# A GRU with a ternary feed-forward network: half group sums ahead of the transposes, a bias seed from ScalarE, and another division of the last tile but one

## The reference, cut to what matters

```python
gi = x @ W_ih + b_ih;  gh = h @ W_hh + b_hh
r = sigmoid(i_r + h_r);  z = sigmoid(i_z + h_z)
n = tanh(i_n + r * h_n)
h_new = (1.0 - z) * n + z * h
...
scale = clip(mean(abs(w_g)), 1e-08)          # groups of 64
w_hat = clip(round(w_g / scale), -1, 1) * scale
gate, up = split(states @ w_gate_up_hat)     # hidden size 1024
h = silu(gate) * up
hn = h * rsqrt(mean(h * h) + eps)            # over the 1024 hidden features
out = x + hn @ w_proj_hat
```

## Time and profile before

| what | us |
|---|---|
| median of 3 runs (354.89 to 356.31) | 355.58 |
| the profiled execution | 355.06 |
| its span, first to last instruction | 353.2 |
| PE busy in the span | 343.9 (97%) |
| DVE busy | 230.1 (65%) |
| ACT busy | 212.8 (60%) |
| POOL busy | 172.5 (49%) |
| the lone steps, transposes of step 0 to those of step 7 | 38.0 |

### The profile page before, as it was taken

How to read it: one execution, slowest core, us unless ns; L and a number is a source line. 1 busy time by engine, 2 the same in 40 slices (tenths; PEclk the granted TensorE clock), 3 DMA queues, 4 the chain that set the end, 5 groups by cost and what they waited for, 6 DMA issues and landing times.

```text
span 353.2 us, 5445 instructions
## 1 busy us (share of the span) xinstructions
PE 343.9 (97%) x2026; PEld 298.5 (84%) x2031; DVE 230.1 (65%) x438; ACT 212.8 (60%) x408; POOL 172.5 (49%) x144
## 2 busy tenths in 40 slices
PE   7999999999999999999999999999999999999994
PEld 3788887888888888888888889888898888898894
DVE  6788887899666655656648554675656545744655
ACT  4776767876747566456646656366565556645651
POOL 1022121176735447255363447445462556889882
PEclk9999999999999999999999999999999999999999
DMA  6990000017001000220001000010001000010101
GB/s 226 385 416 16 2 1 2 0 45 314 1 2 59 0 3 1 75 105 1 2 0 61 0 2 0 0 62 1 2 0 59 2 0 2 1 59 2 59 2 60
DMA packets 5570, 17.92 MB, mean 51 GB/s; under 512 B 420, under 2 KB 2084, under 8 KB 5032
## 3 DMA queue, kind: packets, MB, share of 16 engines
q1 hardware_dynamic: 5544, 17.58, 13.1%
HBM read 13.38 MB, written 4.19 MB: 50 GB/s over the span
## 4 chain that ended last, share of the span: by engine, by line
PE 81%; DVE 9%; ACT 3%; issue 2%; DMA 2%; SPq 1%; DVEq 0%
PE ps_ffn L819 29%; PE ps_out L854 16%; PE ps_rz L750 6%; PE ps_rz L751 6%; PE ps_rz L755 6%; PE ps_n L750 3%; PE ps_n L751 3%; PE ps_n L755 3%; PE ps_t L812 2%; DMA x_ring<-in_L_ffn_w_gate_up_dram 2%; PE ps_rz L819 2%; PE ps_t L865 2%; DVE zm_n L519 1%; DVE h_nat L522 1%; DVE o_st L602 1%
## 5 line engine op out<-in xcount | busy, mean ns | idle before, releaser
L285 POOL TENSOR_TENSOR hid_lo<-work,hid_hi 128x512 fp32r<-128x512 f32 x62 | 81.2, 1309 | 112.3 <-ACT hid_hi L352 112.3
L819 PE MATMUL ps_ffn<-st_hi,wguT 128*128 128x512 f32 x236 | 93.3, 395 | 0.3 <-DVE work L536 0.3
L819 PE MATMUL ps_ffn<-st_lo,wguT 128*128 128x512 f32 x236 | 92.6, 392 | 0.0
L292 POOL TENSOR_TENSOR sq_sum<-sq_sum,work 128x512 f32<-128x512 f32 x55 | 74.2, 1349 | 0.4 <-ACT work L364 0.4
L536 DVE TENSOR_TENSOR work<-work,ps_ffn 128x512 f32<-128x512 f32 x55 | 37.7, 685 | 32.8 <-ACT work L348 32.0
L819 PEld LDWEIGHTS ps_ffn<-st_hi,wguT 128*128 128x128 f32 x236 | 44.4, 188 | 8.5 <-DVE work L536 1.0
L819 PEld LDWEIGHTS ps_ffn<-st_lo,wguT 128*128 128x128 f32 x236 | 44.4, 188 | 7.4
L546 DVE TENSOR_TENSOR work<-work,ps_ffn 128x512 f32<-128x512 f32 x63 | 43.2, 686 | 8.2 <-PE ps_ffn L819 6.6
L352 ACT CAST hid_hi<-work 128x512 fp32r<-128x512 f32 x63 | 38.8, 616 | 16.1 <-DVE work L546 16.1
L854 PEld LDWEIGHTS ps_out<-wpT,hid_hi 128*128 128x128 f32 x252 | 37.3, 189 | 4.6 <-DVE o_st L563 1.0
L854 PE MATMUL ps_out<-wpT,hid_hi 128*128 128x256 f32 x252 | 40.5, 283 | 0.1
(11 more groups left out here) (166 smaller groups left out, 681.1 us busy)
## 6 DMA issues: line engine op xcount, KB each, us to landing
out_dram<-o_st SPq DMA_DIRECT2D x7, 512.0 KB, 2.6
xT_all<-in_x_dram SPq DMA_DIRECT2D x1, 3072.0 KB, 17.9
x_ring<-in_x_dram SPq DMA_DIRECT2D x1, 3072.0 KB, 11.4
x_ring<-in_L_ffn_w_gate_up_dram SPq DMA_DIRECT2D x4, 512.0 KB, 9.8
x_ring<-in_L_ffn_w_proj_dram SPq DMA_DIRECT2D x2, 512.0 KB, 10.1
x_ring<-in_x_dram SPq DMA_DIRECT2D x1, 1024.0 KB, 5.6
work<-in_L_cond_W_ih_dram SPq DMA_DIRECT2D x2, 384.0 KB, 4.5
work<-in_L_cond_W_hh_dram SPq DMA_DIRECT2D x2, 384.0 KB, 6.1
```

What stands on the lines that cost most here:

```text
L285: nc.gpsimd.tensor_tensor(hid_lo[:, j % RING], hid[:, j % 2], f32(hid_hi[:, j % RING]), ALU.subtract).then_inc(hid_lo_ok, 1)
L292: nc.gpsimd.tensor_tensor(sq_sum[:], sq_sum[:], hid_sq[:, j % 2], ALU.add).then_inc(sq_added, 1)
L819: mm = pe.matmul(bank, w, group_state(part, G, k), start=(k == 0 and i == 0), stop=(k == KD - 1 and i == 1))
```

## The change

- The group sums of unit u = 1 to 4 are split: the first half (`halves=(0,)`) goes into odd step t = 2u-1, ahead of that step's transposes; the second half into step 2u, after its state product. In the same steps ACT's quantiser operations change places: signs of unit u in even step 2u after the r gate, final weights of unit u-1 in the odd step there, means of unit u in the even step after tanh. `q_sign` gets two buffers.
- The bias of the n gate for steps 3 to 8 is written by ACT (`seed_n(t+2)` in steps 1 to 6, after `input_hi`), where PE did it with two matmuls.
- POOL's low part of input t waits for the r gate of step t-1 besides its high part.
- At the end POOL makes the low part of tile 6 and doesn't add its square; DVE adds that square to `sq_sum`, between `last_hidden("a")` and `last_gated("b")`, and doesn't make that low part. ACT squares half a of tile 7. PE takes `T6` ahead of `Ta`.

```diff
-          "U5", "D3", "G6", "U6", "D4", "Ga", "Ua", "D5", "Gb", "Ub", "Ta", "T6", "Tb", "D6", "Da", "Db"]
+          "U5", "D3", "G6", "U6", "D4", "Ga", "Ua", "D5", "Gb", "Ub", "T6", "Ta", "Tb", "D6", "Da", "Db"]
...
                 pool.wait_ge(x_hi, t + 1)
+                pool.wait_ge(r_ok, min(t, LEAD))
                 nc.gpsimd.tensor_tensor(xT_lo[:, t % 2], xT_all[:, :, t, :], f32(xT_hi[:, t % 2]),
...
             def tile(G, j):
                 n = 8 * G + j
-                if n < NG * HT - 2:
-                    pool.wait_ge(hid_hi_ok, n + 1)
+                pool.wait_ge(hid_hi_ok, n + 1)
...
-                if j:
+                if j and n < NG * HT - 2:
                     pool.wait_ge(hid_sq_ok, n + 1)
...
             def seed_n(t):
-                act.wait_ge(n_pre_ok, t)
-                nc.scalar.copy(ps_n[:], bias[:, 1, :]).then_inc(n_seed, 1)
+
+                act.wait_ge(n_pre_ok, t - 1 if t <= LEAD else t)
+                nc.scalar.copy(n_bank(t), bias[:, 1, :]).then_inc(n_seed, 1)
...
                 r_gate(t)
-                if odd:
+                if t == 0:
+                    bias_tile()
+                elif odd and u:
+                    q_weights(u - 1)
+                else:
                     q_signs(u)
-                elif u:
-                    q_means(u)
-                else:
-                    bias_tile()
                 z_gate(t)
                 n_gate(t)
                 if odd:
                     q_abs_of(u + 1)
                 elif u:
-                    q_weights(u - 1)
+                    q_means(u)
...
                 input_hi(t + 2)
+                if 0 < t < LEAD - 1:
+                    seed_n(t + 2)
...
             last_silu("a")
             hidden_square(G, 6)
+            last_hi("a")
             last_silu("b")
-            last_hi("a")
+            act.wait_ge(sq_added, 7 * NG - 2)
+            nc.scalar.activation(hid_sq[:, 1, 0:2 * P], hid[:, 1, 0:2 * P], ACT.Square).then_inc(sq_last, 1)
             last_hi("b")
...
-            j = HT - 2
-            dve.wait_ge(hid_hi_ok, HT * NG - 1)
-            dve.wait_ge(hid_lo_ok, HT * NG - 2)
-            nc.vector.tensor_tensor(hid_lo[:, j % RING], hid[:, j % 2], f32(hid_hi[:, j % RING]),
-                                    ALU.subtract).then_inc(hid_lo_ok, 1)
             last_gated("a")
             last_hidden("a")
-            last_square("a")
+            dve.wait_ge(sq_added, 7 * NG - 2)
+            dve.wait_ge(hid_sq_ok, HT * NG - 1)
+            nc.vector.tensor_tensor(sq_sum[:], sq_sum[:], hid_sq[:, 0], ALU.add).then_inc(sq_added, 1)
             last_gated("b")
             last_hidden("b")
-            last_square("b")
+            last_square()
...
             for t in range(LEAD):
                 if t:
                     state_product(t)
+                if t and t % 2 == 0:
+                    q_group_sums(t // 2, (1,))
                 seed_rz(t + 1)
                 input_rz(t + 1)
-                seed_n(t + 1)
+                if t < 2:
+                    seed_n(t + 1)
                 if t == 0:
                     pe.wait_ge(bias_ok, 2)
+                if t % 2:
+                    q_group_sums((t + 1) // 2, (0,))
                 transpose_state(t)
                 input_n(t + 1)
-                if t % 2:
-                    q_group_sums((t + 1) // 2)
...
                 state_product(t)
+                if t == LEAD:
+                    q_group_sums(4, (1,))
```

More of the change, by code:

```diff
@@ L98, in gru_ffn @@
         q_abs = sb("q_abs", [P, 2, 2, 512], BF16)
-        q_sign, q_mean, q_scale, q_keep, q_kept, q_signed = (
-            sb(n, [P, 2, 512], BF16) for n in ("q_sign", "q_mean", "q_scale", "q_keep", "q_kept", "q_signed"))
+        q_mean, q_scale, q_keep, q_kept, q_signed = (
+            sb(n, [P, 2, 512], BF16) for n in ("q_mean", "q_scale", "q_keep", "q_kept", "q_signed"))
+        q_sign = sb("q_sign", [P, 2, 2, 512], BF16)
         q_ones = sb("q_ones", [P, P], BF16)
@@ L282, in tile @@
                 n = 8 * G + j
-                if n < NG * HT - 2:
-                    pool.wait_ge(hid_hi_ok, n + 1)
-                    nc.gpsimd.tensor_tensor(hid_lo[:, j % RING], hid[:, j % 2], f32(hid_hi[:, j % RING]),
-                                            ALU.subtract).then_inc(hid_lo_ok, 1)
-                if j:
+                pool.wait_ge(hid_hi_ok, n + 1)
+                nc.gpsimd.tensor_tensor(hid_lo[:, j % RING], hid[:, j % 2], f32(hid_hi[:, j % RING]),
+                                        ALU.subtract).then_inc(hid_lo_ok, 1)
+                if j and n < NG * HT - 2:
                     pool.wait_ge(hid_sq_ok, n + 1)
@@ L386, in q_signs @@
             def q_signs(u):
-                if u:
-                    act.wait_ge(q_signed_ok, u)
-                nc.scalar.activation(q_sign[:], unit_part(u, wgu, wpj), ACT.Sign).then_inc(q_sign_ok, 1)
+                if u >= 2:
+                    act.wait_ge(q_signed_ok, u - 1)
+                nc.scalar.activation(q_sign[:, u % 2], unit_part(u, wgu, wpj), ACT.Sign).then_inc(q_sign_ok, 1)
             def q_weights(u):
@@ L581, in last_hidden, with last_square @@
                 nc.vector.tensor_tensor(hid[:, 1, cols], gsg[:, 1, cols], up_from, ALU.mult).then_inc(hid_ok, 1)
-            def last_square(half):
-                cols, _, _, n = last_tile(half)
+            def last_square():
+                cols, _, _, n = last_tile("b")
                 dve.wait_ge(hid_ok, n)
-                dve.wait_ge(sq_added, (HT - 1) * NG - 2)
+                dve.wait_ge(sq_last, 1)
                 nc.vector.tensor_tensor(hid_sq[:, 1, cols], hid[:, 1, cols], hid[:, 1, cols],
@@ L592, in last_lo @@
                 dve.wait_ge(hid_hi_ok, n)
+                dve.wait_ge(hid_lo_ok, HT * NG - 1)
                 nc.vector.tensor_tensor(hid_lo[:, RING - 1, cols], hid[:, 1, cols], f32(hid_hi[:, RING - 1, cols]),
@@ L622, in signed @@
                     dve.wait_ge(q_w_ok, u)
-                nc.vector.tensor_tensor(q_signed[:], q_kept[:], q_sign[:], ALU.mult).then_inc(q_signed_ok, 1)
+                nc.vector.tensor_tensor(q_signed[:], q_kept[:], q_sign[:, u % 2], ALU.mult).then_inc(q_signed_ok, 1)
             nc.vector.memset(q_keep[:], 0.0).then_inc(warm_ok, 1)
@@ L783, in input_n @@
             def input_n(t):
-                if t > LEAD:
-                    pe.wait_ge(n_seed, t - LEAD)
+                if t > 2:
+                    pe.wait_ge(n_seed, t - 2)
                 dst, cols = n_bank(t)[:, 0:D], slice(2 * D, G3)
@@ L893, in last_squares @@
                 if part == "a":
-                    pe.wait_ge(ms_ok, NG - 1)
                     pe.wait_ge(sq_last, 1)
@@ L898, in last_squares @@
                 else:
+                    pe.wait_ge(ms_ok, NG - 1)
                     pe.wait_ge(sq_added, 7 * NG - 1)
@@ L902, in last_squares @@
                     mm = pe.matmul(ps_sq[:, s:s + 1], squares[:, s * P:(s + 1) * P], ones[:],
-                                   start=(s == 0 and part == "a"), stop=part == "b" or (part == "6" and s < 2),
+                                   start=(s == 0 and part == "6"), stop=part != "6",
                                    skip_group_check=True)
@@ L906, in last_squares, with q_group_sums @@
                     mm.then_inc(sq_tok, 1)
-            def q_group_sums(u):
+            def q_group_sums(u, halves=(0, 1)):
                 pe.wait_ge(q_abs_ok, u + 1)
@@ L911, in q_group_sums @@
                     pe.wait_ge(q_mean_ok, u)
-                for a in range(2):
+                for a in halves:
                     mm = pe.matmul(q_sums[:, a], q_ones[:], q_abs[:, u % 2, a, :], start=True, stop=True)
-                mm.then_inc(q_sum, 1)
+                if 1 in halves:
+                    mm.then_inc(q_sum, 1)
             def ffn_item(G, item):
```

1 line of the change is left out of this document (removed).

## The result

The changed kernel takes 352.99 us (median of 11 runs, 352.58 to 354.47), the kernel before 355.42 us in the same comparison (median of 11, 354.60 to 356.81). The ratio, taken over all of these runs, is 0.9939 with a 95% interval of 0.9924 to 0.9954: 0.6% faster (the two medians alone would give 0.9932). The profiled execution has a span of 351.0 us where the one of before had 353.2.

What follows compares the result with a forecast made beforehand. PE was busy 97% of the span; only lone steps and the last 15 us had other engines on the chain. Gains of 1.68 + 0 + 0 + 0.2 = 1.9 us from 355.6 gave 353.7 us, range 352.9 to 354.9.

Steps and rivals of the forecast that it cites:

- Group sums: Lone steps: group sums no longer delay PE's product, 4 x 0.42 = 1.68 us gained in steps 2, 4, 6 and 8.
- its cover: Step 8: PE's pause of 0.29 us was to hold the second half sum's 0.21 us; without it, at most 0.21 us lost.
- The half sum in the odd step: Ahead of odd steps' transposes: |w| ends in time as tanh moves earlier; 0, bounds +0.1 to -1.0 us for four steps.
- rival A: Odd steps: the half sum holds the transposes, 0.15 to 0.26 us in each of four, 354.5 us; chance 0.22.
- The seed on ACT: Steps 1 to 6: ACT's 0.58 us copy fits ahead of the r gate with some 0.2 us to spare; cost 0.
- rival D: Even steps: the product isn't released, low part or r gate behind the seed being next; half of 1.68 us, 354.5 us; chance 0.1.
- The room for the half sums: Steps 2 to 7: two bias matmuls fewer on PE, about 0.23 us, leave room ahead of the transposes; 0 by itself.
- POOL and the ports: Lone steps: POOL held for the r gate, `kept` and `signed` take 0.68 us, not 1.11; by itself worth nothing in odd steps.
- rival B: Lone steps: POOL's hold moves onto z*h, 0.9 us in each of eight steps, 360.9 us; chance 0.05.
- The end: Last 15 us: added sum ends 0.55 us behind POOL, `T6` starts earlier; gain 0.2 us, bounds 0.8 gained to 0.3 lost.
- Rival C: End: the added sum gets the ports ahead of POOL or the low part is shorter; 0.6 us more, 353.1 us; chance 0.1.

Runs made afterwards that it cites:

- no_pool_wait: The changed kernel without POOL's wait for the r gate ahead of its low part of the input: 353.91 us, ratio 0.9947 to the kernel before.
- both_ahead: The changed kernel with both half sums ahead of the odd step's transposes, none split off: 354.13 us, ratio 0.9967 to the kernel before.
- both_behind: The changed kernel with both half sums behind the even step's state product, step 8 included: 352.82 us, ratio 0.9913 to the kernel before.
- pe_seeds: The changed kernel with the n gate's bias seeds of steps 3 to 8 back on PE: 353.42 us, ratio 0.9933 to the kernel before.
- pool_on_zh: The changed kernel with POOL's low part of the input held until the n gate's sum is done: 358.94 us, ratio 1.0101 to the kernel before.
- add_first: The changed kernel with POOL's low part of tile 6 held until DVE's added square sum is done: 352.81 us, ratio 0.9921 to the kernel before.
- end_only: The kernel before with only the change's new end, its lone steps as before: 355.27 us, ratio 0.9982 to the kernel before.

## Why the prediction was right

The forecast was 353.7 us, within 352.9 to 354.9; 352.99 came, only 0.1 us above the lower bound. The mechanism held part by part, as follows. That the median still fell inside the range is in part luck: it hung on how many of the eleven runs met the late fall of the clock, which no term of the sum had counted.

**Group sums.** Expected 4 x 0.42 us, measured 1.81 us over steps 1 to 8: 0.43 to 0.45 us in steps 2, 4 and 6, 0.42 us in step 8 and 0.01 to 0.03 us in each odd step. For step 8 the prediction misread its cover. The 0.29 us of the earlier trace rows are idle time of the weight load; PE's own last matmul ahead of the transposes begins at 60.74, 0.25 us before them, and each such matmul takes 0.23 us from start to start, so PE had no pause there. The half sum then holds the transposes' matmul by 0.17 us, as said above, but the long stretch gives it back, so the 0 for its cost came out by luck. That the z gate sets the step, and PE's product the z gate, is what made the odd step's length the target for the even one, and it was met within 0.03 us (5.23 to 5.25 for 5.26).

**The half sum in the odd step.** Expected 0, with tanh 3.62 us behind the transposes (30.69 - 27.07). It came 30.07 - 26.44 = 3.63 us behind them, and |w| ended 4.99 us behind where 4.98 was worked out. `no_pool_wait` shows that this needs POOL's wait, 1.0 us in all, and `both_ahead` shows that there is no room for a second half (rival A: its price is real, 0.2 us a half, its condition isn't met). `both_behind` shows that the place isn't needed: with no half sum in the odd steps the stretch up to half b is as long. So the wait for |w| was of the change's own making.

**The seed on ACT.** Expected 0 with 0.2 us to spare; 0.26 us are left ahead of the r gates (rival D is out), and `pe_seeds` shows that it brings 0. "The room for the half sums", as the prediction also called it, was too much: they have room without it, since PE waits for |w| anyway.

**POOL and the ports.** The row with 1.11 against 0.68 us was read rightly. The Trainium skill (SBUF — State Buffer, Who interferes with whom) says that the port pair that the two engines share is an exclusive lock, and that issue order decides who blocks. The traces agree in both orders. With POOL first, DVE waits: z*h takes 0.91 for 0.43 us in `pool_on_zh`, and the added sum 1.44 us where `add_first`, which keeps POOL away from it, has 0.68. With DVE first, POOL waits: before the change it began at 33.56 beside `quantised`, begun at 33.55, and took 1.27 us, where it takes 0.72 us in `pool_on_zh` with nothing ahead of it. The prediction's estimate that POOL's low part takes 1.27 us by itself was too high. It was 0.80 us in the change, since some 0.5 us of the 1.27 had been POOL's own wait for DVE; so z*h was safer than rival B had it. What the prediction left out is who waits for that low part: PE's `input_rz`, ahead of all of its passes. In the change POOL ends at 28.87 + 0.80 = 29.67, 0.15 us ahead of the input product's first matmul, which goes at 29.82, straight behind PE's bias matmul and without a wait. Had POOL taken 1.27 us from there, to 30.14, that product would have been some 0.4 us late, which the pauses of 0.54 and 0.51 us ahead of the half sum and the transposes would still have held. So the 0 of this term was safe, but by luck, for this waiter had not been counted; `pool_on_zh` shows what it costs beyond the pause. The Trainium skill (GPSIMD Engine Reference, 3.1 Elementwise) gives some 2.6 cycles an element at 1.2 GHz, by which 256 elements more should cost 0.55 us, an estimate. The traces agree: 1.28 us for 512 elements (`add_first`) less 0.72 us for 256 (`pool_on_zh`) is 0.56 us, which leaves 0.16 us for each instruction.

**The end.** Expected 0.2 us with the added sum blocked to 0.55 us behind POOL's end; it ended 0.54 us behind it, and 0.22 us came. Rival C's gain is real too, but only once POOL is made to wait: 0.46 us in `add_first`.

**What was off.** The sum against the profiled execution was 1.9 us and the spans differ by 2.2, of which 0.19 is the earlier arrival of the first weights. The step that missed is the last one of the sum: the 0.5 us between the profiled execution and the median of before was carried over to the changed kernel as if it were fixed. The profiled execution of before had a clock of 1.00 to the end. Most other executions of that kernel had not: beside the experiments, 33 of its 45 runs have a mean clock of 0.995 or less. Of the change's eleven runs six lie in the lower group, so its median lies there, and 355.06 - 1.9 = 353.2 us would have been nearer to it (352.6 to 353.0). Compared like with like the sum holds: the twelve of these 45 runs with a clock of 0.999 or more have a median of 354.9 us and the change's five such runs one of 352.9, 2.0 us apart. Whether the change itself makes the fall rarer wasn't tested; over all runs here it can't be told from chance.

## What to carry to other kernels

When two kinds of steps alternate, cut the trace at the same event in both: what the longer kind does between the same two events is the gain to be had, and the shorter kind is the limit that it will meet. Look at every pair of VectorE and GpSimd instructions that overlap with two SBUF inputs on VectorE; here one GpSimd start moved by 1.2 us, to a place where VectorE reads PSUM, was worth 1.0 us while two bias matmuls a step taken off TensorE were worth nothing, and moved on to the wrong place it cost 6 us, more than the whole change brings. Ask also who waits for the instruction that is moved. Near the end, put real work that is ready ahead of tiny matmuls and not behind them, since here what stood behind them ran at half the clock in about half of the executions.

## What was not expected of the hardware

The granted clock falls to 1.2 GHz in the last microseconds of many runs, during or behind 1.8 us of one-column matmuls (at about 345.7 us in the trace of `pe_seeds`), with a pause of 0.7 us ahead of them or without one (`add_first`), and costs about 1.2 us (353.8 to 354.5 against 352.6 to 353.0 us). With five useless matmuls of 512 columns ahead of and between them no run of six showed the loss, nor did one with the down product of tile 6 moved ahead of them. The earlier the fall, the more it costs: in the profiled execution of `both_behind`, at 354.98 us 2.2 us above the median of its kernel, it comes at about 345.1, while the one-column matmuls still run. Why it comes in some executions of a kernel and not in others stays open.

The recorded clock can also be low at no visible cost. In the profiled execution of `end_only` it is 0.95, neither of the two levels, in every stretch from 6 us to 350 us, and yet transposes of step 0 to step 8 take 44.91 us (44.85 before) and the long stretch behind them 282.77 us (282.63).

Another thing is how such delays show: the weight load of a late matmul may be recorded on time (31.76 in `both_ahead`) while the matmul itself is late (31.98), so that a step's loss appears in the next step when the cuts are made at weight loads. The same holds for step 8 of the changed kernel (58.99 and 59.16).
